# A two-layer attention and expert kernel: own memory for the stacks' parts, late constants, loads of 24 or 25 rows, unread dense products, maxima 13 tiles ahead

## The chip, the cores and the metric

The kernel runs on one core of a Trainium2 chip. The metric is the time of one execution on the device in microseconds (us). Before the change three runs took 2064.13, 2058.0 and 2061.1 us, a median of 2061.1. The profiled execution is a fourth one.

## What is computed

Two transformer layers work on x of shape (2, 1024, 128), all in float32:

```
x = x + attn0(layernorm(x))              # rotary embedding, 16 heads of 8
x = x + ffn0(layernorm(x))               # 1 shared and 7 routed experts, top 2
x = x + attn1(layernorm(x))              # own norm, biases, softmax(q k / sqrt 8) v
x = x + ffn1(layernorm(x))               # relative-position attention, then 32 experts, top 4

def attn0: q, k, v = split(x @ Wqkv); q, k = rope(q), rope(k)
           attn = softmax(q k^T * 8**-0.5); return (attn v) @ Wo
```

For two sequences and 16 heads each attention has 32 (sequence, head) pairs, called heads below. Each has 1024 queries, 1024 keys and a width of 8.

## The kernel before

The program is ten stages, each written once for every engine: `front(0)`, `attention(0)`, `front(1)`, `experts0`, `front(2)` (with `back(0)` ahead of it), `attention(1)`, `front(3)`, `relative_attention`, `front(4)`, `experts1`. Every engine runs its own list in the order written, and semaphores tie the lists together. No scheduler reorders anything. TensorE is `e` under `@block.tensor`, VectorE (DVE) under `@block.vector`, ScalarE (ACT) under `@block.scalar`, GpSimd (POOL) under `@block.gpsimd`; SyncE (SP) issues all DMAs in one queue.

**A front** works on four groups of 512 tokens. DVE normalizes rows, TensorE transposes them, ACT copies the transpose to `XT`, and TensorE multiplies it with the weights (`proj_ok`). In front(0) DVE rotates k and q (L1091 to L1101: two products with `rope`, one sum, each). Every q and k value is split into a rounded high part and a low remainder: ACT writes the high part (`khi_ok`, `qhi_ok`), POOL (front 0, L1690 and L1693) or DVE the low one. These parts live in `hls`, two buffers in turn, the second inside `PR`. `q_out` (L330) and `k_out` (L341) store them to `q_stack` and `k_stack` in DRAM as 24 rows a head; rows 24 to 31 come from `in_pad`, and row 24 of the k stack holds ones.

**An attention's head** is loaded by `load_qk` (L366): eight DMAs of 32 rows, four copies of q and four of k, into slot s of `Qs` and `Ks`. Three things then happen to a head. Its maxima: `scores` (L624, L630) makes a tile of 128 queries by 1024 keys in two of four PSUM banks, and DVE takes the negated row maximum (L1212); eight tiles a head. Its maxima's row: `max_row` (L637) transposes the eight columns, ACT copies them to `MT` (L1474), and `max_rows` (L383) sends them by two DMAs into row 24 of two of the head's q copies, so that the next product has the maximum subtracted already. Its `position`: sixteen `turned` products (L645) with keys along the partitions, ACT's exponentials (L1486), and `values` (L655), three key tiles behind. `scores` may be two tiles ahead of DVE, `turned` three products ahead of ACT. A position starts with the wait for its own maxima's row (`m_in`). The lead is two heads: 16 tiles of scores go before position 0, and position n carries the scores of head n+2, one tile for each of its eight steps. In step 1 it has `max_row` for head n+1, and in step 2 it waits until ACT has copied that row.

TensorE begins an attention after `products_read`, that is once every product of the front has been read out of PSUM, and in attention 0 after the constants have come (`c_in`). The constants and the pad rows are issued by SP at the program's start (L320 to L327). ACT's first maxima's row waits until all parts are stored (`stacks_stored`), because `PR` holds some of them.

Of the kernel before, what the change touches and what calls it, by code (L numbers as in the profile page):

```python
# [24 lines left out]
P = 128  # L25
# [62 lines left out]
def two_layers(nc, A, out):  # L88
    with ExitStack() as ctx:
# [79 lines left out]
        kin = [qk[:, 1, :], PR[:, 2, 0:GW]]  # L169
        hl0, hl0_r = two("hl", [P, 2, 2, GW])  # L170
        hls = [hl0_r, PR_r[:, 0:2, :].rearrange("p a (b t) -> p a b t", b=2)]
# [60 lines left out]
        qin_ok = sem("qin_ok")  # L232
        kin_ok, split_q, lgt_ok, ex_in, ex_ok, gate_ok, gtp_ok, gt_ok = map(
# [14 lines left out]
        pad_in, khi_ok, qhi_ok = map(sem, "pad_in khi_ok qhi_ok".split())  # L248
# [38 lines left out]
        RING = [0, 1, 7]  # L287
        TURN = [[0, 1], [4, 5]]
        FIRST = [2, 0, 4]
        MEETINGS = [3, 4, 9, 10]  # L290
        GATE_BANK = [3, 5, 1, 2]
        EARLY = (0, GT * (NG - 1))
# [18 lines left out]
        def _(e):  # L311
# [8 lines left out]
            for d, src, w in ((q_stack, 0, L), (k_stack, 1, L), (w_stack, 0, 2 * P)):  # L320
                e.dma_start(d[:, MROW:KR, :], A["pad"][src:src + 1, :, 0:w].broadcast_to([NH, KR - MROW, w]))\
                    .then_inc(pad_in, 16)
            loads = [(w_qkv[:, 1:3, :], A["w_qkv"][:, 1:3, :]), (w_out[:], A["w_out"]), (cols[:], A["cols"]),
                     (rows[:], A["rows"]), (rel[:], A["rel"][:, 1:3, :]), (w_rt0[:], A["w_rt0"]), (w_rt1[:], A["w_rt1"])]
            for dst, src in loads:
                e.dma_start(dst, src).then_inc(c_in, 16)
            assert len(loads) == N_CONST  # L327

            def q_out(a, g):

                b, half = g // 2, g % 2
                if a == 0:
                    e.wait_ge(split_q, g + 1)
                else:
                    e.wait_ge(qin_ok, 4 * a + g + 1)
                d = q_stack[b * H:(b + 1) * H, :, half * GW:(half + 1) * GW]
                for c in range(TERMS):
                    e.dma_start(d[:, c * DH:(c + 1) * DH, :], hls[g % 2][:, 0, Q_PARTS[c], :].bitcast(F32))\
                        .then_inc(stq_out[half], 16)

            def k_out(a, g):  # L341
# [6 lines left out]
                for c in range(TERMS):  # L348
                    e.dma_start(d[:, c * DH:(c + 1) * DH, :], hls[g % 2][:, 1, K_PARTS[c], :].bitcast(F32))\
# [16 lines left out]
            def load_qk(n, s):  # L366
                for to, of in ((Qs_r, q_stack), (Ks_r, k_stack)):
                    for r in range(4):
                        e.dma_start(to[r * KR:(r + 1) * KR, s, :].bitcast(F32), of[bass.ds(n, 1)].rearrange("n r t -> (n r) t"))\  # L369
                            .then_inc(qk_in[s], 16)  # L370

            def load_rel(n, s):
                load_qk(n, s)
                e.dma_start(Ws_r[WROW, s, :].bitcast(F32), w_stack[bass.ds(n, 1)].rearrange("n r t -> (n r) t")).then_inc(ws_in[s], 16)

            def attention(a):
# [21 lines left out]
                max_rows(0, 0)  # L398
                load(3, 3)
# [4 lines left out]
                position(NH - 3, 1, False)  # L404
                if a == 1:
# [34 lines left out]
            def experts0():  # L440
# [6 lines left out]
                for x in range(1, NE0 - 2):  # L447
                    e.wait_ge(w0_ok, x + 1)
                    load_expert(0, x + 2, x % 2)
                    e.wait_ge(xw_ok, NG * x)  # L450
# [17 lines left out]
            def front(f):  # L468
# [8 lines left out]
                for g in range(NG):  # L477
# [3 lines left out]
                    if g == 2:  # L481

                        for half in range(2):
                            e.wait_ge(stq_out[half], 16 * TERMS * (2 * a + 1))
                            e.wait_ge(stk_out[half], 16 * TERMS * (2 * a + 1))
                        e.wait_ge(pad_in, 16 * 3)
                        if f == 3:
                            e.wait_ge(w_out_ok, 16 * 6)
                            load_rel(0, 0)
                        else:  # L490
                            load_qk(0, 0)
                    q_out(a, g)
                    k_out(a, g)
                    if g == 2:
                        for n in range(1, 3):
                            if f == 3:
                                load_rel(n, n)
                            else:
                                load_qk(n, n)
                if f in QKV:  # L500
                    for half in range(2):
                        e.wait_ge(stq_out[half], 16 * TERMS * 2 * (QKV.index(f) + 1))
                        e.wait_ge(stk_out[half], 16 * TERMS * 2 * (QKV.index(f) + 1))
# [30 lines left out]
        def _(e):  # L534
# [18 lines left out]
            def front(f):  # L553
# [24 lines left out]

                if a is not None:
# [5 lines left out]
                for g in range(NG):  # L585
# [4 lines left out]
                    e.wait_ge(xn_ok, u + 1)  # L590
                    if a2 is None:
                        e.wait_ge(xh_ok, 4 * (f // 4) + g)
                    for t in range(GT):
                        m = transpose(PS[:, 0, t * P:(t + 1) * P], xn[:, t, :])
                    m.then_inc(xT_ok, 1)
# [3 lines left out]
                    if a2 is not None:  # L599
                        products_read(4 * a2 + g)  # L600
                        for w, bk in ((2, 3), (3, 4), (0, 1), (1, 2)):
                            if f == 0 or w % 2 == 0:
                                e.matmul(bank(bk), w_qkv[:, a2, w * P:(w + 1) * P], xT(f, g), start=True, stop=True)\
                                    .then_inc(proj_ok, 1)
                        for t in range(GT):
# [15 lines left out]

            def attention(a):
                HB = NH * a

                def scores(n, s, qt):

                    e.wait_ge(max_done, 8 * (HB + n) + qt + 1)
                    for kh in range(2):
                        rows_ = slice((2 + kh) * KR, (3 + kh) * KR)
# [1272 lines left out]
```

## Time and profile before

| | us |
|---|---|
| median of three runs | 2061.1 |
| profiled execution, its own time | 2062.49 |
| its span, first to last instruction | 2060.5 |
| front 0, to TensorE's first score | 46.4 |
| attention 0, to the last output copy | 322.1 |
| attention 1, from its first score | 331.6 |
| relative attention and the rest after 980.3 | 1080.2 |

The profile's page gives the busy time of each engine, the span in 40 slices, the DMA queues, the chain that ended last and the costliest groups. A row of the timeline gives start and length in us, engine, line, operation, what is written from what, how many instructions, and in brackets the idle time before it with what ended it. "PEld" is a weight load, "SPq" a DMA issue. An f32 product is two instructions.

### The profile page before, as it was taken

The page shows a single profiled execution, that of the slowest core. Times are in us where ns is not written, and L with a number is a line of the kernel's source. Part 1 is how long each engine was busy: PE and PEld are TensorE (multiplying, and loading weights), DVE is VectorE, ACT ScalarE, POOL GpSimd, SP SyncE. Part 2 cuts the span into 40 slices and gives each one's busy share as a digit, 9 for nine tenths or more (in the row PEclk, how much of TensorE's full clock was granted, in tenths as well). Part 3 has the DMA queues.
Part 4 walks back from the last instruction along what each step waited for, and adds up shares of the span by engine and source line. Part 5 has one row for each costly group of instructions (what it writes and reads, how often), then busy time and mean ns, then how long its engine had stood idle before and what let it go on. Part 6 is the DMA issues. An engine that isn't in the chain of part 4 may idle for free.

```text
span 2060.5 us, 40384 instructions
## 1 busy us (share of the span) xinstructions
PE 1918.0 (93%) x13792; PEld 1159.1 (56%) x13792; DVE 1382.8 (67%) x1778; ACT 1205.9 (59%) x2289; POOL 507.2 (25%) x493
## 2 busy tenths in 40 slices
PE   5999999799985999999689999999999999977998
PEld 2333333577762333333356666666666666665887
DVE  6999997556658899996565455555555555346776
ACT  2699999466652799999224444444444444433553
POOL 2000000178862100000222222222222222103654
PEclk8799999899996799999799999999999999988999
DMA  8444542121106445453512211111112211014554
GB/s 275 135 129 127 129 128 77 60 88 63 52 0 196 113 119 134 123 136 86 170 52 60 58 48 50 47 48 47 47 51 61 51 50 47 8 33 179 213 218 144
DMA packets 90189, 198.58 MB, mean 96 GB/s; under 512 B 19872, under 2 KB 49312, under 8 KB 84768
## 3 DMA queue, kind: packets, MB, share of 16 engines
q1 hardware_dynamic: 90080, 197.10, 32.5%
q8 instruction: 71, 1.16, 0.2%
q14 instruction: 38, 0.31, 0.1%
HBM read 162.42 MB, written 36.18 MB: 96 GB/s over the span
## 4 chain that ended last, share of the span: by engine, by line
PE 46%; DVE 2%; DMA 1%; SPq 1%; issue 0%; ACT 0%; DVEq 0%
PE PS L749 17%; PE PS L833 8%; PE PS L761 6%; PE PS L735 6%; PE PS L744 4%; PE PS L724 4%; DVE M L1233 1%; SPq L369 1%; DMA Ks<-in_kv 0%; DMA Ws_r<-w_stack 0%; PE PS L768 0%; PE PS L575 0%; PE PS L707 0%; PE PS L566 0%; PE PS L545 0%
## 5 line engine op out<-in xcount | busy, mean ns | idle before, releaser
L1212 DVE TENSOR_REDUCE M<-PS 128x1 f32<-128x1024 f32 x512 | 595.1, 1217 | 23.0 <-PE PS L630 17.6
L1486 ACT ACTIVATE PR<-PS 128x512 f32<-128x512 f32 x1024 | 539.2, 602 | 41.7 <-PE PS L645 21.3
L1522 ACT ACTIVATE PR<-PS 128x512 f32<-128x512 f32 x512 | 305.8, 598 | 378.5 <-PE PS L749 374.7
L1233 DVE TENSOR_REDUCE M<-PS 128x1 f32<-128x1024 f32 x256 | 311.8, 1221 | 218.4 <-PE PS L735 211.3
L655 PE MATMUL PS<-PR,Va 128*32 128x256 f32 x4096 | 332.2, 397 | 15.6 <-POOL Va L1669 2.7
L645 PE MATMUL PS<-Qs_r,Ks_r 32*128 32x512 f32 x1024 | 310.6, 508 | 0.5 <-ACT PR L1486 0.4
L630 PE MATMUL PS<-Ks_r,Qs_r 32*128 32x512 f32 x1024 | 269.6, 524 | 23.0 <-DVE M L1212 10.3
L630 PEld LDWEIGHTS PS<-Ks_r,Qs_r 32*128 32x128 f32 x1024 | 99.6, 192 | 228.4 <-issue 153.2
L1228 DVE TENSOR_TENSOR rt<-PS,rel 128x512 f32<-128x512 f32 x128 | 88.4, 691 | 162.5 <-PE PS L707 160.9
L655 PEld LDWEIGHTS PS<-PR,Va 128*32 128x32 f32 x4096 | 83.5, 108 | 149.7 <-ACT PR L1486 62.0
L1669 POOL TENSOR_TENSOR Va<-Vt,nil 128x64 f32<-128x64 f32 x96 | 27.8, 293 | 536.7 <-PE PS L655 533.3
L749 PE MATMUL PS<-BIG_r,Eh 128*128 128x512 f32 x512 | 159.4, 393 | 0.0
L1750 POOL TENSOR_TENSOR qk<-rt 128x512 f32<-128x512 f32 x64 | 82.4, 1287 | 277.9 <-DVE rt L1228 277.9
L645 PEld LDWEIGHTS PS<-Qs_r,Ks_r 32*128 32x128 f32 x1024 | 133.1, 185 | 26.7 <-ACT PR L1486 11.1
L1776 POOL TENSOR_TENSOR BIG_r<-BIG,BIG_r 128x512 fp32r<-128x512 f32 (+1 forms) x96 | 128.3, 1342 | 49.0 <-ACT BIG_r L1554 48.7
L761 PE MATMUL PS<-PR,Va 128*32 128x256 f32 x2048 | 136.8, 385 | 0.0
L1289 DVE TENSOR_TENSOR BIG<-PS,SRC 128x512 f32<-128x512 f32 (+1 forms) x96 | 65.9, 688 | 86.0 <-PE PS L833 85.8
L833 PE MATMUL PS<-Ah,PR_r 128*128 128x512 f32 x376 | 116.4, 391 | 0.0
L833 PE MATMUL PS<-BIG_r,PR_r 128*128 128x512 f32 x384 | 108.0, 390 | 4.5 <-POOL BIG_r L1814 3.3
L749 PEld LDWEIGHTS PS<-BIG_r,Eh 128*128 128x128 f32 x512 | 96.1, 188 | 21.3
L749 PE MATMUL PS<-BIG_r,El 128*128 128x512 f32 x256 | 101.1, 395 | 0.0
L749 PE MATMUL PS<-Ah,Eh 128*128 128x512 f32 x256 | 100.8, 394 | 0.0
(204 smaller groups left out, 3034.8 us busy)
## 6 DMA issues: line engine op xcount, KB each, us to landing
Qs_r<-q_stack SPq DMA_DIRECT2D x384, 128.0 KB, 2.6
Ks_r<-k_stack SPq DMA_DIRECT2D x384, 128.0 KB, 3.1
Qs<-g_dram SPq DMA_DIRECT2D x29, 1024.0 KB, 4.7
o_dram<-Ob SPq DMA_DIRECT2D x96, 128.0 KB, 2.0
Ks<-g_dram SPq DMA_DIRECT2D x10, 1024.0 KB, 4.8
q_stack<-hl_r SPq DMA_DIRECT2D x18, 256.0 KB, 3.3
k_stack<-hl_r SPq DMA_DIRECT2D x18, 256.0 KB, 4.1
q_stack<-PR_r SPq DMA_DIRECT2D x18, 256.0 KB, 3.2
```

What stands on the lines that cost most here:

```text
L630: m = e.matmul(bank(2 + 2 * (qt % 2) + kh), Qs_r[rows_, s, qt * P:(qt + 1) * P], Ks_r[rows_, s, kh * GW:(kh + 1) * GW], start=True, stop=True)
L645: e.matmul(bank(RING[(x + turn) % 3]), Ks_r[rows_, s, kt * P:(kt + 1) * P], Qs_r[rows_, s, qh * GW:(qh + 1) * GW], start=True, stop=True). ...
L655: m = e.matmul(PS[32 * g:32 * g + VC, 6, 0:256], Va[:, s, kt, :], PR[:, kt % 4, g * 256:(g + 1) * 256], start=(kt == 0), stop=(kt == QT - 1))
L735: m = e.matmul(bank(bk + kh), q[:, qt * P:(qt + 1) * P], k[:, kh * GW:(kh + 1) * GW], start=first, stop=not first)
L749: m = e.matmul(bank(TURN[kt % 2][qh]), e_part[:, kt * P:(kt + 1) * P], a_part[s][:, qh * GW:(qh + 1) * GW], start=False, stop=(k == 2))
L761: m = e.matmul(PS[32 * g:32 * g + VC, 6, 0:256], Va[:, s, kt, :], PR[:, kt % 4, g * 256:(g + 1) * 256], start=(kt == 0), stop=(kt == QT - 1))
L833: m = e.matmul(out, w[a], h[b], start=start and n == 0, stop=n == 2 or not start, skip_group_check=not start)
L1212: e.tensor_reduce(M[:, s, qt:qt + 1], PS[:, 2 + 2 * (qt % 2):4 + 2 * (qt % 2), :] .rearrange("p a b -> p (a b)"), AX.X, ALU.max, negate=Tr ...
L1233: e.tensor_reduce(M[:, s, qt:qt + 1], PS[:, bk:bk + 2, :].rearrange("p a b -> p (a b)"), AX.X, ALU.max, negate=True).then_inc(max_done, 1)
L1486: e.activation(PR[:, kt % 4, qh * GW:(qh + 1) * GW], bank(RING[(x + turn) % 3]), ACT.Exp, scale=SCALE).then_inc(exp_done, 1)
L1522: e.activation(PR[:, kt % 4, qh * GW:(qh + 1) * GW], bank(TURN[kt % 2][qh]), ACT.Exp)\
L1776: e.tensor_tensor(h0p[0:w, 1, tg % 2, c, :], h0[0:w, c, :], h0p[0:w, 0, tg % 2, c, :].bitcast(F32), ALU.subtract).then_inc(lo_ok, 1)
```

## The change

1. The parts of front 0 get four buffers of their own in `BIG`, those of front 2 three of four; `stacks_stored` goes from attentions 0 and 1.
2. In front 0 POOL takes over the two sums of the rotation, TensorE transposes group g+1 in the middle of group g's products, and ACT copies that transpose ahead of group g's parts.
3. The constants are issued at the end of attention 0, the pad rows in experts0. Only the row of ones is sent at the start.
4. In attentions 0 and 1 q is loaded with 24 rows, k with 25, and the products use 24 (scores) or 25 rows (turned). Heads 0 and 1 are loaded ahead of group 2's stores, head 2 ahead of group 3's.
5. `keep_warm` multiplies weights by weights into PSUM that nobody reads: 26 products of 128 columns before attention 0's first score, 28 before attention 1's, one of 256 columns after each of the 13 leading tiles, and one in each of the first three steps of position 0.
6. The lead is 13 tiles (NEAR = 5 of head 1). Position n carries tiles 5 to 7 of head n+1, then 0 to 4 of head n+2. `max_row` moves from step 1 to step 4, the wait for its copy from step 2 to step 5, and ACT's copy from before exponential 4 to before exponential 10.

```diff
+        wide = BIG_r[:].rearrange("p (g a b t) -> p g a b t", g=NG, a=2, b=2)
+        PAIR = [hl0_r, PR_r[:, 0:2, :].rearrange("p a (b t) -> p a b t", b=2)]
+        HL = {0: [wide[:, g] for g in range(NG)],
+              2: [hl0_r, wide[:, 2], wide[:, 3], hl0_r],
+              3: [PAIR[g % 2] for g in range(NG)]}
...
SP:
-            for d, src, w in ((q_stack, 0, L), (k_stack, 1, L), (w_stack, 0, 2 * P)):
+            def constants():      # 7 DMAs, at the end of attention 0
+            def pads():           # 3 DMAs, in experts0
+            e.dma_start(k_stack[:, MROW:MROW + 1, :], ...).then_inc(one_in, 16)
...
-            def load_qk(n, s):
+            def load_qk(n, s, q_depth=MROW, k_depth=MROW + 1):
...
                 max_rows(0, 0)
+                if a < 2:
+                    stored(2 * (a + 1))
                 load(3, 3)
...
                 position(NH - 3, 1, False)
+                if a == 0:
+                    constants()
...
TensorE, front 0:
+                            if f == 0 and w == 0:
+                                if g + 1 < NG:
+                                    turn_rows(g + 1)
+                                e.wait_ge(qrot_ok, g)
...
+            def keep_warm(n, bk=7, cols_=256):
+                for _ in range(n):
+                    e.matmul(PS[:, bk, 0:cols_], w_qkv[:, 0, 0:P], w_qkv[:, 0, 0:cols_], start=True, stop=True)
...
TensorE, position:
                     for kt in range(QT):
-                        if ahead:
-                            if kt == 0:
+                        if kt < QT - NEAR and n + 1 < NH:
+                            scores(n + 1, (s + 1) % SLOTS, NEAR + kt)
+                        if kt >= QT - NEAR and n + 2 < NH:
+                            if kt == QT - NEAR:
                                 e.wait_ge(qk_in[s2], ...)
-                            scores(n + 2, s2, kt)
+                            scores(n + 2, s2, kt - (QT - NEAR))
                         turned(n, s, 2 * kt, turn)
                         turned(n, s, 2 * kt + 1, turn)
-                        if kt == 2 and rows_next:
+                        if first and kt in FREE6:
+                            keep_warm(1, 6)
+                        if kt == 5 and n + 1 < NH:
                             e.wait_ge(mt_copied, HB + n + 2)
...
-                        if kt == 1 and rows_next:
-                            max_row(n + 1, (s + 1) % SLOTS, alone=first)
+                        if kt == 4 and n + 1 < NH:
+                            max_row(n + 1, (s + 1) % SLOTS)
...
+                keep_warm([26, 28][a], cols_=P)
                 products_read(4 * (a + 1))
-                if a == 0:
-                    e.wait_ge(c_in, 16 * N_CONST)
                 for n in range(2):
                     e.wait_ge(qk_in[n], 128 * (NH // SLOTS * a + 1))
-                    for qt in range(QT):
+                    for qt in range([QT, NEAR][n]):
                         scores(n, n, qt)
+                        keep_warm(1)
...
ACT:
-                        if x == 4 and rows_next:
+                        if x == 10 and rows_next:
                             max_copy(n + 1, (s + 1) % SLOTS)
...
-                stacks_stored(a)
+                if a == 0:
+                    e.wait_ge(split_k, NG)
+                    e.wait_ge(split_q, NG)
...
POOL, front 0:
+                        e.tensor_tensor(kin[g % 2], rt[:, 0, :], rt[:, 1, :], ALU.add).then_inc(kin_ok, 1)
+                        e.tensor_tensor(qk[:, 0, :], rtq[:, 0, :], rtq[:, 1, :], ALU.add).then_inc(qin_ok, 1)
```

TensorE's list where front 0 ends and attention 0 begins, before (L606 is the last product of the front, L630 the scores, L637 the maxima's row, L645 the turned products, L655 the values):

```order
L606 MATMUL PS<-w_qkv,XT 128x128 x4
L630 MATMUL PS<-Ks_r,Qs_r 128x512 x20
L637 MATMUL PS<-ident,M 8x128
L630 MATMUL PS<-Ks_r,Qs_r 128x512 x14
L645 MATMUL PS<-Qs_r,Ks_r 128x512 x2
```

The same place in the changed kernel (L649, L678 and L685 are the same functions; L668 is `keep_warm`):

```order
L649 MATMUL PS<-w_qkv,XT 128x128 x4
L668 MATMUL PS<-w_qkv 128x128 x26
L678 MATMUL PS<-Ks_r,Qs_r 128x512 x2
L668 MATMUL PS<-w_qkv 128x256
L678 MATMUL PS<-Ks_r,Qs_r 128x512 x2
```

The dense products stand ahead of the first score and between the tiles; 13 tiles go before the first turned product instead of 16 (a 17th stood in position 0's first step).

TensorE's list in position 0, before, from the last leading tile on:

```order
L630 MATMUL PS<-Ks_r,Qs_r 128x512 x14
L645 MATMUL PS<-Qs_r,Ks_r 128x512 x2
L630 MATMUL PS<-Ks_r,Qs_r 128x512 x2
L645 MATMUL PS<-Qs_r,Ks_r 128x512 x2
L637 MATMUL PS<-ident,M 8x128
L630 MATMUL PS<-Ks_r,Qs_r 128x512 x2
```

and after, steps 2 to 5 of position 0 (L693 turned, L703 values):

```order
L668 MATMUL PS<-w_qkv 128x256
L678 MATMUL PS<-Ks_r,Qs_r 128x512 x2
L693 MATMUL PS<-Qs_r,Ks_r 128x512 x2
L703 MATMUL PS<-PR,Va 32x256 x4
L678 MATMUL PS<-Ks_r,Qs_r 128x512 x2
L693 MATMUL PS<-Qs_r,Ks_r 128x512 x2
L703 MATMUL PS<-PR,Va 32x256 x4
L685 MATMUL PS<-ident,M 8x128
L678 MATMUL PS<-Ks_r,Qs_r 128x512 x2
```

The row of the next head's maxima stands three steps later in a position than it did.

SP's list around the first loads, before:

```order
L349 DMA k_stack<-PR_r 16x8x512 x3
L369 DMA Qs_r<-q_stack 32x1024 x4
L369 DMA Ks_r<-k_stack 32x1024 x4
L338 DMA q_stack<-hl_r 16x8x512 x3
L349 DMA k_stack<-hl_r 16x8x512 x3
L369 DMA Qs_r<-q_stack 32x1024 x4
```

and after:

```order
L366 DMA k_stack<-BIG_r 16x8x512 x3
L386 DMA Qs_r<-q_stack 24x1024 x4
L386 DMA Ks_r<-k_stack 25x1024 x4
L386 DMA Qs_r<-q_stack 24x1024 x4
L386 DMA Ks_r<-k_stack 25x1024 x4
L355 DMA q_stack<-BIG_r 16x8x512 x3
```

Head 1's loads now stand ahead of group 2's stores, and each DMA has fewer rows.

## Rows read from the trace of the kernel before

**Rows 1.** The page, part 2: granted TensorE clock in 40 slices of 51.5 us.
```profile
PEclk8799999899996799999799999999999999988999
```
**Rows 2.** Windows, by stage: stretch, us, busy of PE, PEld, DVE, ACT, POOL, clock, DMA share, GB/s.
```profile
46.40:368.50 322.10, 308.41 (x3140) 120.10 (x3141) 298.06 (x257) 284.11 (x577) 12.67 (x41) 0.96 0.46 123
648.70:980.30 331.60, 313.70 (x3140) 120.83 (x3141) 298.85 (x257) 284.51 (x577) 17.55 (x34) 0.93 0.47 127
```
**Rows 3.** Windows inside the two attentions.
```profile
46.35:74.30 27.95, 22.14 (x88) 7.82 (x88) 25.25 (x22) 8.06 (x15) 4.54 (x13) 0.51 0.59 170
74.30:349.00 274.70, 267.23 (x2870) 104.54 (x2867) 271.80 (x234) 258.33 (x527) 8.18 (x28) 1.00 0.47 123
...
648.70:669.00 20.30, 12.47 (x34) 4.56 (x34) 18.28 (x16) 1.55 (x2) 0.42 (x1) 0.50 0.86 256
669.00:695.60 26.60, 24.20 (x156) 7.59 (x160) 16.95 (x14) 15.74 (x31) 9.23 (x7) 0.50 0.36 97
```
**Rows 4.** Timeline of DVE at attention 0's start.
```profile
46.92 20.45 DVE L1212 TENSOR_REDUCE M<-PS 128x1 f32<-128x1024 f32 x18 [1.90 <-PE PS L630]
67.72 2.35 DVE L1212 TENSOR_REDUCE M<-PS 128x1 f32<-128x1024 f32 x2 [0.35 <-PE PS L630]
```
**Rows 5.** Timeline of DVE at attention 1's start.
```profile
649.57 9.14 DVE L1212 TENSOR_REDUCE M<-PS 128x1 f32<-128x1024 f32 x8 [2.63 <-PE PS L630]
...
671.78 2.35 DVE L1212 TENSOR_REDUCE M<-PS 128x1 f32<-128x1024 f32 x2 [2.90 <-PE PS L630]
```
**Rows 6.** Timeline of front 0: a group's value products, POOL, first loads, first score.
```profile
24.14 1.05 PE L606 MATMUL PS<-w_qkv,XT 128*128 128x128 f32 x8
...
27.34 1.26 POOL L1693 TENSOR_TENSOR PR_r<-qk,PR_r 128x512 fp32r<-128x512 f32 x1 [1.29 <-ACT PR_r L1396]
...
28.28 3.70 PE L603 MATMUL PS<-XT,w_qkv 128*128 128x512 f32 x8 [2.65 <-ACT XT L1438]
...
35.68 1.74 SPq L369 DMA_DIRECT2D Qs_r<-q_stack  x4
...
46.38 0.74 PE L630 MATMUL PS<-Ks_r,Qs_r 32*128 32x512 f32 x4 [3.43 <-DVEq L1208]
```
**Rows 7.** Timeline of front 2: first loads, last product, first score of attention 1.
```profile
641.99 1.73 SPq L369 DMA_DIRECT2D Qs_r<-q_stack  x4
...
643.58 1.05 PE L606 MATMUL PS<-w_qkv,XT 128*128 128x128 f32 x8
...
648.74 1.22 PE L630 MATMUL PS<-Ks_r,Qs_r 32*128 32x512 f32 x4 [4.10 <-DMA Ks_r<-k_stack]
```
**Rows 8.** Timeline of attention 0's end.
```profile
339.67 9.48 DVE L1212 TENSOR_REDUCE M<-PS 128x1 f32<-128x1024 f32 x8
...
366.16 1.93 PE L655 MATMUL PS<-PR,Va 128*32 128x256 f32 x32
```
**Rows 9.** Timeline of one position in the middle of attention 0.
```profile
207.20 1.72 SPq L369 DMA_DIRECT2D Qs_r<-q_stack  x4
...
207.45 0.50 PE L630 MATMUL PS<-Ks_r,Qs_r 32*128 32x512 f32 x2
...
209.56 0.38 PE L637 MATMUL PS<-ident,M 128*8 128x128 f32 x2
...
210.20 0.25 ACT L1474 ACTIVATE MT<-PS 8x128 fp32r<-8x128 f32 x1
...
212.18 1.34 SPq L383 DMA_DIRECT2D Qs_r<-MT  x2
...
216.84 0.50 PE L630 MATMUL PS<-Ks_r,Qs_r 32*128 32x512 f32 x2
```
**Rows 10.** Windows at the loads' end and after that row's DMAs (columns of group 2).
```profile
213.00:213.50 0.50, 0.50 (x9) 0.16 (x8) 0.50 (x1) 0.50 (x3) 0.00 (x0) 1.00 0.18 55
214.50:214.75 0.25, 0.25 (x7) 0.13 (x3) 0.25 (x1) 0.25 (x2) 0.00 (x0) 1.00 0.04 12
214.75:215.00 0.25, 0.25 (x4) 0.21 (x4) 0.25 (x1) 0.25 (x2) 0.00 (x0) 1.00 0.00 0
```
**Rows 11.** DMA queue from 641 to 652: packets, MB, share of 16 engines.
```profile
q1 hardware_dynamic: 1266, 2.66, 79.9%
```

More of the change, by code:

```diff
@@ L319, in _ @@
             e.dma_start(rope[:], A["rope"]).then_inc(rope_in, 16)
-            for d, src, w in ((q_stack, 0, L), (k_stack, 1, L), (w_stack, 0, 2 * P)):
[L321 to L327, printed above, removed]
+            def constants():
+                loads = [(w_out[:], A["w_out"]), (cols[:], A["cols"]), (rows[:], A["rows"]),
+                         (w_rt0[:], A["w_rt0"]), (w_rt1[:], A["w_rt1"]),
+                         (w_qkv[:, 1:3, :], A["w_qkv"][:, 1:3, :]), (rel[:], A["rel"][:, 1:3, :])]
+                for dst, src in loads:
+                    e.dma_start(dst, src).then_inc(c_in, 16)
+                assert len(loads) == N_CONST
+            def pads():
+                for d, src, w in ((q_stack, 0, L), (k_stack, 1, L), (w_stack, 0, 2 * P)):
+                    e.dma_start(d[:, MROW:KR, :], A["pad"][src:src + 1, :, 0:w].broadcast_to([NH, KR - MROW, w]))\
+                        .then_inc(pad_in, 16)
+            e.dma_start(k_stack[:, MROW:MROW + 1, :], A["pad"][1:2, 0:1, 0:L].broadcast_to([NH, 1, L])).then_inc(one_in, 16)
             def q_out(a, g):
@@ L481, in front @@
                     if g == 2:
[L483 to L486, printed above, removed]
+                        stored(2 * a + 1)
                         if f == 3:
+                            e.wait_ge(pad_in, 16 * 3)
                             e.wait_ge(w_out_ok, 16 * 6)
@@ L490, in front @@
                         else:
+                            e.wait_ge(one_in, 16)
                             load_qk(0, 0)
+                            load_qk(1, 1)
+                    if g == 3 and f < 3:
+                        load_qk(2, 2)
                     q_out(a, g)
                     k_out(a, g)
-                    if g == 2:
+                    if g == 2 and f == 3:
                         for n in range(1, 3):
[L496 to L503, printed above, removed]
+                            load_rel(n, n)
+                if f == 3:
+                    stored(2 * (QKV.index(f) + 1))
             def attention1():
@@ L577, in spread, with turn_rows @@
                     m.then_inc(spread_ok, 1)
+                def turn_rows(g):
+                    e.wait_ge(xn_ok, 4 * f + g + 1)
+                    if a2 is None:
+                        e.wait_ge(xh_ok, 4 * (f // 4) + g)
+                    if f == 0:
+                        e.wait_ge(xs_ok, g)
+                    for t in range(GT):
+                        m = transpose(PS[:, 0, t * P:(t + 1) * P], xn[:, t, :])
+                    m.then_inc(xT_ok, 1)
+                if f == 1:
+                    e.wait_ge(c_in, 16 * N_CONST)
                 if a is not None:
@@ L589, in front @@
                         spread(3)
[L590 to L595, printed above, removed]
+                    if f > 0 or g == 0:
+                        turn_rows(g)
                     if g:
@@ L657, in values, with position @@
                     m.then_inc(pv_done, 1)
-                def position(n, block, s, turn, first=False, ahead=True, rows_next=True):
+                def position(n, block, s, turn, first=False):
                     s2 = (s + 2) % SLOTS
@@ L693, in attention @@
                 for n in range(1, NH):
-                    position(n, n // SLOTS, n % SLOTS, n % 3, ahead=n < NH - 2, rows_next=n < NH - 1)
+                    position(n, n // SLOTS, n % SLOTS, n % 3)
                 for kt in range(QT - 3, QT):
@@ L1402, in projected @@
                         else:
[L1403 removed]
+                            e.activation(HL[f][g][:, 1, 0, :], bank(3), ACT.Copy).then_inc(khi_ok, 1)
                         e.wait_ge(proj_ok, pr + 2)
[L1405 removed]
+                        if f == 3:
+                            e.wait_ge(stq_out[half], 16 * TERMS * (2 * a2 + g // 2))
+                        elif g == 3:
+                            e.wait_ge(stq_out[0], 16 * TERMS * (2 * a2 + 1))
```

98 lines of the change are left out of this document (59 added, 39 removed).

## The prediction

> **What bounds the kernel now.** I read the page's clock line first, because TensorE's clock decides which engine is the bound. In [rows 1] it has a low slice at the start and another at slice 13, counted from 1; at 51.5 us a slice these are the beginnings of the two attentions. The windows by stage come next: [rows 2] give 322.1 us to attention 0 and 331.6 to attention 1, with equal work and clocks of 0.96 and 0.93. Then I cut each attention [rows 3]. From 74.3 to 349.0 the clock is 1.00 and VectorE is busy 271.80 of 274.70 us with 234 maxima, TensorE 267.23, ACT 258.33: three engines in lockstep, 274.70 / 234 × 8 = 9.39 us a head. Before 74.3 the clock is 0.51; from 648.7 to 695.6 it is 0.50, so TensorE ran at 1.2 GHz, not 2.4. There VectorE waits. Last come timelines. VectorE has gaps in both slow stretches [rows 4, 5]. TensorE's first score comes at 46.38, right after the front's last product is read [rows 6], and at 648.74, after a wait of 4.10 us for the first head's loads [rows 7]. At the end the last maximum is taken at 339.67 + 9.48 = 349.15, and the values end at 368.1: 19.0 us in which VectorE has no maxima [rows 8].
>
> So an attention costs its 256 maxima on VectorE (one every 9.39 / 8 = 1.17 us), the gaps at its start, and the tail. The change touches all three and hardly the other stages.
>
> **The change part by part**, summed against the profiled execution's 2062.5 us, which is 1.4 above the median of the three runs.
>
> *Attention 0's start.* The first loads wait for the stores of groups 0 and 1. POOL ends group 1's last part at 27.34 + 1.26 = 28.6, and the loads are issued from 35.68 [rows 6], 7.1 later. Own buffers remove waits of ACT for earlier stores, but POOL gets two more operations a group; at 1.26 each, four are 5.0 us a group. I put group 1's parts at 28.2 to 30.2 and the loads at 35.3 to 37.3. In front 2 a head is there 648.74 − 641.99 = 6.75 us after its first issue [rows 7]: 42.0 to 44.0. TensorE's front may end near 37, since POOL's sums overlap the next group. The 26 dense products follow. Four value products, also of 128 columns (eight instructions), took 1.05 us, 0.26 each; four of 512 columns took 3.70, which is 0.23 for 128 [rows 6]. So 26 are 6.0 to 6.8 us and end at 43 to 43.8. I take the first score at 43.3: −3.0. Bounds: −4.5 (loads at 35.3, no dense product late) and +0.5 (group 1 late behind POOL's five us a group).
>
> *Attention 0's slow stretch.* Of 27.95 us VectorE worked 25.25; 0.57 is the wait for the first tile, so some 2.1 to 2.3 are gaps [rows 3, 4]. With TensorE kept busy they go: at full clock a tile's scores (0.50, [rows 9]) and one dense product of 256 columns (2 × 0.23) are 0.96, under VectorE's 1.17. What is late next is the maxima's row of head 0, for which I keep 0.3: −2.0. Bounds −2.3 and +3.0 (the slow clock stays in part).
>
> *Attention 1's start.* TensorE waited 4.10 us for the loads there, its last front product ending at 644.6 [rows 7]. 28 dense products at 0.23 are 6.4 us: first score at 651.0, +2.3. Bounds 0 and +3.2 (0.26 each); a little comes back if the loads, now of 24 and 25 rows, are quicker, which doesn't help as the dense products end last.
>
> *Attention 1's gaps.* VectorE worked 18.28 of the first 20.30 and 16.95 of the next 26.60 us: 11.67 idle, less 0.87 for the first tile, 10.8 [rows 3]. They hold 2.90 ahead of 671.78 [rows 5], where ACT's first row waited for the parts' stores, and that wait is gone. I keep 0.7: −10.1. Bounds −10.8 and 0.
>
> *Tail.* The lead is 13 tiles, so after the last maximum there are three tiles' time less. At full clock the tail's 19.0 us are two heads of 16 tiles [rows 8], 1.19 a tile, of which a little is a fixed end; at 1.13 a tile three are 3.4, for each attention: −6.8. Bounds −7.2 and −5.
>
> *Steady state.* The scores and turned products are as many as before, in another order; what moves is the maxima's row. In [rows 9] a position begins at 207.45, ACT's copy at 210.20, 2.75 later; three steps of 1.17 make that 6.26 and its end 6.51. SP is free then: its loads are issued from 207.20, and the queue is nearly empty by 213.0 (share 0.18, [rows 10]). Two issues take 1.34, after some 0.16, and the last packets land 1.15 behind the issue, since 212.18 + 1.34 = 213.52 and the share falls to 0.04 and 0.00 by about 214.65 [rows 10]. The row is home at 6.51 + 0.16 + 1.34 + 1.15 = 9.16, and the next position starts at 9.39 [rows 9]: 0.23 to spare. Behind that wait stand TensorE's scores and turned products, thus VectorE and ACT at once; what covers it is VectorE's tile in hand and ACT's two exponentials, about 0.4. I take 0.05 a head over 60 heads: +3. Bounds −3 (the even mix of tiles runs closer to VectorE's 1.16) and +17.
>
> *Constants.* Seven DMAs at attention 0's end stand in SP's queue ahead of the last output stores, some 2 MB at the 2.66 MB in 11 us of [rows 11], so 8 us, beside two heads of computation: +0.5, bounds 0 and +2. The pad rows go out in experts0 between loads of experts, and I give them nothing: the expert in hand hides them, and uncovered they would cost about 2.25 / 2.66 × 11 = 9 us once. Loads of 24 and 25 rows move 23% less beside compute; nothing, since the queue already empties before a position ends [rows 10].
>
> Sum: −3.0 − 2.0 + 2.3 − 10.1 − 6.8 + 3.0 + 0.5 = −16.1, so 2046.4 for a profiled execution, and 2045.0 against the median.
>
> **Rivals.**
>
> *A. The maxima's row is late in every head.* For: only 0.23 us to spare, by a chain of five terms. Against: up to 0.4 of cover. At 0.3 us a head over 58 heads it takes back 17 us: 2062, the same as before.
>
> *B. The clock doesn't hold, slower than before.* For: in the slow stretch of attention 1 TensorE was busy 24.20 of 26.60 us and its clock was 0.50 all the same [rows 3], so busy time alone doesn't bring the high clock. If it stays low through the leading tiles, a tile is its scores (0.74 then, [rows 6]) and a dense product at half speed (0.92), about 1.7 us against VectorE's 1.13 with no gap: 13 × 0.57 = 7.5 an attention, 15 in both, and the savings of the gaps (12.1) don't come: −16.1 + 27.1 = +11.0, 2072. It decides from the point where the clock is still 0.5 at the sixth or seventh tile. Against: the dense products leave no idle time ahead of the first score, and in the steady state a busy TensorE has 1.00 [rows 3].
>
> *C. Loads of 24 and 25 rows use fewer DMA engines.* Now 32 rows go over 16 engines, a head's 1 MB being 64 KB on each, and [rows 11] give 2.66 MB / 11 us / 0.8 / 16 = 19 KB a us and busy engine: 3.4 us a head. If the rows were spread over 12 and 5 engines, the busiest five would carry 4 × 8 + 4 × 20 = 112 KB, 5.9 us. That lies inside a head's 9.39, so steadily nothing unless the maxima's row has to queue behind it; loads seen from 207.20 on would then end near 214.2, when that row is issued. The first head comes up to 2.5 later in attention 0 (+2.5) and 0.5 in attention 1: 2048. The Trainium skill, "DMA: Bandwidth & Descriptors", section "Why a DMA increments its semaphore by 16 and not by 1", says that the number of engines is the largest up to 16 that divides both sides' outer sizes, which gives 12 for 24 rows and 5 for 25. No row here has a load of 24 or 25 rows.
>
> *D. More gain.* Front 0 by the lower bound, the steady state at −3: 2045.0 − 1.5 − 6 = 2037.5. It belongs to the forecast's range.
>
> **How the numbers follow.** Forecast with D 0.60, A 0.14, B 0.12, C 0.14. A measurement tells about 0.3%, 6.2 us, from no change. Forecast and C lie under 2054.9 but for a small part of each; A is split between the same and a little slower or faster, B is slower. Faster: 0.57 of the forecast, 0.14 of C, 0.03 of A, 0.74. Same: 0.03 of the forecast, 0.08 of A and 0.01 of B, 0.12. Slower: 0.11 of B and 0.03 of A, 0.14. The forecast's own range is 2036 to 2053: the front's, the tail's and the steady state's ends, which are not all met at once. To leave out 2 in 10 it reaches into A, to 2062, and on the low side to 2032 for a steady state better than I can bound. B stays outside.
>
> **What would show it.** Right: the first score near 43 and 651; the clock 1.00 from the first tile or a few later; VectorE's gaps in the first 25 us of each attention under 1 us in all; the last maximum to the end of values 15.6 us instead of 19.0; a head in the steady state 9.39 to 9.45. Wrong: TensorE idle at a position's start with the wait for the row's DMA named there (A); 0.5 in the windows of the leading tiles (B); a DMA share near 5/16 while a head is loaded (C). The forecast fails if a steady head is above 9.6 or the leading 13 tiles take over 19 us.

## The result and the profile after

The change made the kernel slower. Sixteen runs have a median of 2094.6 us (2066.0 to 2113.0) against 2064.8 of the kernel before (16 runs, 2058.0 to 2069.3); the ratio is 1.011 with a 95% interval of 1.009 to 1.013, taken without the five longest runs, whose clocks were lowest (0.937 to 0.944), while the two medians are 1.4% apart. Time and mean granted clock go together over the runs: 0.968 at 2066.0 us, 0.953 at 2088.2, 0.937 at 2113.0. The profiled run took 2106.1 us (span 2104.3, clock 0.941), so the sizes read from it are those of a longer run.

Where the 43.8 us between the two spans (2104.3 and 2060.5) lie, read from the timelines:

| us | before | after | difference |
|---|---|---|---|
| first score of attention 0 | 46.4 | 44.3 | −2.1 |
| to attention 0's last maximum | 302.8 | 327.9 | +25.1 |
| its tail, to the last values | 18.9 | 15.6 | −3.4 |
| to attention 1's first score | 280.6 | 287.2 | +6.6 |
| to attention 1's last maximum | 312.2 | 327.4 | +15.2 |
| its tail | 18.9 | 15.6 | −3.4 |
| the rest | 1080.6 | 1086.3 | +5.7 |

The clock line of the page, beside [rows 1], is low over two slices at the start of each attention (slices 2 and 3, 13 and 14, counted from 1, of 52.6 us each); the low slice 21 lies behind attention 1, as slice 20 did before:

```profile
PEclk9579999799998599999979999999999999988999
```

The windows (columns as in [rows 2]), cut where the clock changes:

```profile
44.30:60.00 15.70, 14.27 (x54) 6.40 (x54) 14.79 (x13) 1.55 (x2) 2.77 (x8) 1.00 0.78 271
60.00:128.30 68.30, 66.88 (x440) 20.55 (x440) 45.31 (x37) 42.35 (x82) 1.17 (x4) 0.50 0.22 69
128.30:365.00 236.70, 231.74 (x2457) 93.30 (x2456) 228.71 (x200) 219.87 (x451) 7.04 (x24) 1.00 0.31 98
675.03:677.80 2.77, 2.77 (x11) 1.38 (x12) 2.24 (x2) 0.00 (x0) 0.00 (x0) 1.00 1.00 336
677.80:735.80 58.00, 58.00 (x284) 20.09 (x283) 39.12 (x33) 25.44 (x48) 9.92 (x8) 0.50 0.35 113
735.80:957.70 221.90, 216.58 (x2296) 87.09 (x2294) 213.98 (x188) 205.47 (x421) 6.76 (x23) 1.00 0.32 100
957.70:967.90 10.20, 10.20 (x74) 2.94 (x70) 6.95 (x6) 6.76 (x14) 0.29 (x1) 0.50 0.24 78
```

Attention 0 starts as forecast: 13 maxima in 15.7 us at 2.4 GHz. Then come 68.3 us at 1.2 GHz in which VectorE takes 37 maxima; at 1.17 us each they would need 43.3, so 25.0 are lost. Attention 1 loses 58.0 − 33 × 1.17 = 19.4, and 10.2 − 6 × 1.17 = 3.2 in a third stretch. Before, the stretches at 1.2 GHz were 27.3 and 47.8 us long, and the first of them lay mostly over the lead, where VectorE still set the pace: its 22 maxima in 27.95 us [rows 3] lost 27.95 − 22 × 1.17 = 2.2. Now TensorE, not VectorE, is the bound: busy 58.00 of 58.00 us in attention 1, and the clock stays down.

What stood ahead of the first fall, from the timeline of TensorE and SP:

```profile
55.13 0.39 PE L685 MATMUL PS<-ident,M 128*8 128x128 f32 x2
...
55.93 1.90 SPq L406 DMA_DIRECT2D Qs_r<-MT  x2
...
57.99 0.70 PE L668 MATMUL PS<-w_qkv 128*128 128x256 f32 x2
...
61.42 0.79 PE L678 MATMUL PS<-Ks_r,Qs_r 24*128 24x512 f32 x2 [2.73 <-DMA Qs_r<-MT]
```

Head 0's maxima's row is made after the tenth tile, at 55.13. Three tiles follow, and TensorE then stands 2.73 us until the row is home at 61.4. The clock falls at 60.0, inside that wait. The other two falls have a wait ahead of them as well, in attention 1 for the first head (fall at 677.8), in its steady state for a row (957.38 is a position's start, the fall is at 957.7):

```profile
665.16 2.63 SPq L386 DMA_DIRECT2D Qs_r<-q_stack  x4
...
675.03 0.49 PE L678 MATMUL PS<-Ks_r,Qs_r 24*128 24x512 f32 x2 [1.27 <-DMA Ks_r<-k_stack]
...
678.53 0.79 PE L678 MATMUL PS<-Ks_r,Qs_r 24*128 24x512 f32 x2
679.25 1.22 PE L668 MATMUL PS<-w_qkv 128*128 128x256 f32 x2
...
957.38 0.55 PE L678 MATMUL PS<-Ks_r,Qs_r 24*128 24x512 f32 x2 [1.14 <-DMA Qs_r<-MT]
```

The view of TensorE's waits (us in total, times, longest) has seven for the row; before there was one, of 3.5 us.

```profile
PE PS L678 <- DMA Qs_r<-MT: 6.9, 7, 2.7
```

### The profile page after: what moved, and what is told of

It is laid out like the page before. It is cut to its first block, busy times and chain, and to the rows that moved or that the text cites. A ratio compares the mean times of both kernels' runs of the same rounds, so it can differ in the third digit from the quotient of the medians.

```text
span 2104.3 us, 40783 instructions
## 1 busy us (share of the span) xinstructions
PE 1987.1 (94%) x13964; PEld 1197.7 (57%) x13964; DVE 1372.9 (65%) x1770; ACT 1206.8 (57%) x2289; POOL 517.8 (25%) x501
## 4 chain that ended last, share of the span: by engine, by line
PE 46%; DVE 2%; DMA 1%; SPq 1%; issue 0%; ACT 0%; DVEq 0%
PE PS L801 17%; PE PS L885 8%; PE PS L787 6%; PE PS L813 6%; PE PS L796 4%; PE PS L776 4%; SPq L386 1%; DMA Ks<-in_kv 0%; DVE M L1280 0%; DMA Ws_r<-w_stack 0%; PE PS L820 0%; PE PS L600 0%; PE PS L759 0%; PE PS L591 0%; DMA k_stack<-PR_r 0%
## 5 line engine op out<-in xcount | busy, mean ns | idle before, releaser
L703 PE MATMUL PS<-PR,Va 128*32 128x256 f32 x4096 | 351.6, 418 | 7.1 <-POOL Va L1726 3.4
L693 PE MATMUL PS<-Qs_r,Ks_r 25*128 25x512 f32 x1024 | 326.3, 532 | 0.1
L678 PE MATMUL PS<-Ks_r,Qs_r 24*128 24x512 f32 x1024 | 277.4, 537 | 8.4 <-DMA Qs_r<-MT 6.9
L678 PEld LDWEIGHTS PS<-Ks_r,Qs_r 24*128 24x128 f32 x1024 | 101.9, 196 | 231.6 <-issue 112.6
L703 PEld LDWEIGHTS PS<-PR,Va 128*32 128x32 f32 x4096 | 85.2, 111 | 145.2 <-issue 69.0
L693 PEld LDWEIGHTS PS<-Qs_r,Ks_r 25*128 25x128 f32 x1024 | 141.3, 193 | 22.1 <-ACT PR L1542 6.2
L813 PE MATMUL PS<-PR,Va 128*32 128x256 f32 x2048 | 136.8, 385 | 0.0
L1881 POOL TENSOR_TENSOR BIG_r<-BIG,BIG_r 128x512 fp32r<-128x512 f32 x64 | 82.6, 1292 | 73.7 <-ACT BIG_r L1676 71.7
```

What stands on the lines that cost most here:

```text
L678: m = e.matmul(bank(2 + 2 * (qt % 2) + kh), Qs_r[rows_, s, qt * P:(qt + 1) * P], Ks_r[rows_, s, kh * GW:(kh + 1) * GW], start=True, stop=True)
L693: e.matmul(bank(RING[(x + turn) % 3]), Ks_r[rows_, s, kt * P:(kt + 1) * P], Qs_r[rows_, s, qh * GW:(qh + 1) * GW], start=True, stop=True). ...
L703: m = e.matmul(PS[32 * g:32 * g + VC, 6, 0:256], Va[:, s, kt, :], PR[:, kt % 4, g * 256:(g + 1) * 256], start=(kt == 0), stop=(kt == QT - 1))
L813: m = e.matmul(PS[32 * g:32 * g + VC, 6, 0:256], Va[:, s, kt, :], PR[:, kt % 4, g * 256:(g + 1) * 256], start=(kt == 0), stop=(kt == QT - 1))
```

## The experiments

Three theories had to be told apart: the row of maxima comes late and the stall brings the clock down (ROW), products of 24 or 25 rows keep it down longer (ROWS24), the dense products lengthen the lead (DENSE). Each ratio below is to the kernel before, with its 95% interval. One run of each kernel was profiled. The stages behind attention 1 are the same in all kernels, and yet took 1076.9 to 1087.3 us in the profiles (1080.6 before); what two whole spans differ by is therefore not all due to the edit.

**1. The lead of 16 tiles again**, in the changed kernel.

```
NEAR = 8;  max_row in step 1, its wait in step 2;  ACT's copy ahead of exponential 4;  FREE6 = (0, 1)
```

> The changed kernel with its sixth point undone: 16 leading tiles, the maxima's row back in step 1 (two of the three extra dense products in position 0 stay). Theory ROW (the row of maxima comes home after the next position starts, TensorE stalls, its clock falls to 1.2 GHz): no wait for the row's DMA in the steady state, no slow stretch inside an attention, 2050 to 2062 us, with attention 0 at 2.4 GHz from its start. Theory ROWS24 (products of 24 or 25 rows make a slow stretch last longer): slow stretches at the attentions' starts stay at 50 to 70 us, 2080 to 2095. Theory DENSE (the dense products at 1.2 GHz lengthen the lead): little changes, about 2090.

Measured: 2072.9 us, ratio 1.004 (1.001 to 1.008). Attention 0 had no slow stretch, and TensorE waited for no row. Attention 1 had one of 75.1 us, which began 1.4 us after a wait of 1.16 us ahead of position 0. Between the theories: the stalls for rows go, the length of a stretch doesn't.

**2. 32 rows again**, in the changed kernel.

```
def load_qk(n, s, q_depth=KR, k_depth=KR);  rows_ of scores and turned over KR = 32 rows;  pads() at the start
```

> The changed kernel with loads and products of 32 rows in attentions 0 and 1 again, and the pad rows at the program's start, as before the change. Theory ROWS24: once in a position, the 1.2 GHz stretch ends within 7 to 25 us, as before the change; stretches of 30 to 45 us instead of 58 and 68; 2065 to 2075 us. Theory ROW: the stalls at the positions' starts stay or grow a little, as a head's loads are longer, and with them the slow stretches: 2085 to 2105.

Measured: 2066.3 us, ratio 1.000 (0.998 to 1.003): the rows alone give back the whole loss. Eight waits for the row, 9.4 us in all, the longest 3.7: no fewer than with 24 rows. But the stretches that follow are 6.8 and 10.2 us long. From the windows, the lead and the slow stretch of attention 0, then of attention 1:

```profile
46.00:64.60 18.60, 16.35 (x66) 7.57 (x66) 16.34 (x15) 3.06 (x5) 2.08 (x6) 1.00 0.92 274
64.60:71.40 6.80, 6.80 (x38) 2.34 (x36) 4.49 (x4) 4.18 (x9) 0.00 (x0) 0.50 0.44 101
...
654.00:672.20 18.20, 14.54 (x57) 6.52 (x56) 14.79 (x13) 1.55 (x2) 1.83 (x3) 1.00 1.02 320
672.20:682.40 10.20, 10.08 (x48) 3.95 (x48) 6.12 (x5) 5.70 (x11) 7.54 (x4) 0.50 0.27 68
```

**3. No dense products**, in the changed kernel.

```
FREE6 = ();  no keep_warm ahead of the first score or between the tiles
```

> The changed kernel without any dense product. Theory DENSE (they keep TensorE busy without raising its clock, at 1.87 us a tile where VectorE needs 1.2): the lead runs at VectorE's pace, 15 us less in attention 1, about 2080 us. Theory ROW: TensorE idles at the start as before the change and is at 1.2 GHz from the first tile, the 13 leading tiles go by VectorE, then positions run at 1.74 us a tile till the clock comes back; 2085 to 2110, no better than with them.

Measured: 2085.0 us, ratio 1.013 (1.006 to 1.019). Slow from 44.1 for 58.0 us, in attention 1 from 661.9 for 30.7 and from 962.3 for 6.8; waits for the row of up to 5.0 us. By the time DENSE falls: without them it is no better, as the interval takes in the changed kernel's. (In its profile attention 1 needs 311.0 us to the last maximum, 16.4 less than in the changed kernel's, but that one was a longer run.) In one place its mechanism is there all the same. In the changed kernel's attention 1 the ten leading tiles behind the fall come every 1.87 us (678.53 to 680.40), the dense products included, and lose 697.79 − 678.53 − 10 × 1.17 = 7.6 us up to position 0; before, at the same clock, VectorE took a leading tile every 9.14 / 8 = 1.14 us [rows 5].

**4. 24 and 25 rows alone**, in the kernel before; **5. the same with the loads left at 32 rows.**

```
4: to[r*KR : r*KR + depth], of[n, 0:depth];  rows_ over MROW = 24 (scores) and MROW + 1 (turned)
5: only the two rows_
```

> The kernel before the change, with nothing but the loads of 24 and 25 rows and products of as many. Theory ROWS24: the slow stretches at the attentions' starts grow from 27 and 48 us to 50 to 70, 2075 to 2090 us. Theory ROW: nothing changes, 2058 to 2069, as the loads end before a position does.

> The kernel before the change, its loads left at 32 rows, only the products of attentions 0 and 1 over 24 (scores) or 25 rows (turned). This parts the products' rows from the loads'. Theory PRODUCTS (fewer rows in the array hold the clock down longer): as with both, slow stretches of 50 to 80 us at the attentions' starts, 2080 to 2095 us. Theory LOADS (loads of 24 or 25 rows land later or disturb something): no change from before, 2058 to 2070.

Measured: 2094.7 us, ratio 1.012 (1.007 to 1.018), and 2077.4 us, 1.008 (1.004 to 1.011). The row count alone gives a loss as large as the whole change's (four runs in 4), and most of it comes with the products. Whether the loads add something to the time stays open, as the intervals overlap. The slow stretches of 4, then of 5, each with attention 0's first; before they were 27.3 and 47.8 us:

```profile
46.70:125.20 78.50, 71.33 (x428) 22.16 (x428) 59.40 (x50) 39.95 (x77) 5.25 (x16) 0.50 0.30 94
667.90:725.90 58.00, 44.96 (x244) 14.50 (x244) 41.01 (x35) 22.50 (x43) 9.66 (x7) 0.50 0.41 132
```

```profile
49.50:110.90 61.40, 56.18 (x325) 17.75 (x326) 48.52 (x42) 30.50 (x59) 3.77 (x12) 0.50 0.44 117
660.40:745.70 85.30, 73.08 (x440) 22.92 (x440) 60.47 (x52) 40.69 (x79) 10.40 (x10) 0.50 0.49 136
```

**13, 14. One of the two products with fewer rows**, in the kernel before.

```
13: scores over MROW rows;  14: turned over MROW + 1 rows
```

> The kernel before the change, with only the products of the scores over 24 rows instead of 32 (loads and turned products as before). Theory PRODUCTS, in proportion: scores lose 8 of 32 rows, turned products 7 of 32, so each alone lengthens the slow stretches by about half of what both did; 2066 to 2075 us. Rival: only one of the two matters; then this one or the next is at 2058 to 2068 as before and the other at 2072 to 2095.

> The kernel before the change, with only the turned products over 25 rows instead of 32. Theory PRODUCTS, in proportion: about half of the loss, 2066 to 2075 us; the slow stretches at the attentions' starts end 10 to 25 us later than the 27 and 48 us of before. Rival: see the run before.

Measured: 2067.2 us, ratio 1.003 (1.001 to 1.005), and 2065.6 us, 1.001 (0.999 to 1.003). In both profiled runs, the quickest of ten each, the stretches were 34.1 and 41.0 us, 75.1 together, as in the kernel before. Each alone costs a third of the 0.8% of both or less, and for 14 the interval takes in no change: not in proportion, and not one of the two.

**6. One more tile of lead; 7. the hole filled; 8. constants early**, all in the changed kernel with 32 rows.

```
6: NEAR = 6;  max_row in step 3, its wait in step 4;  ACT's copy ahead of exponential 8
7: keep_warm(8) ahead of position 0's first wait
8: constants() at the program's start
```

> The changed kernel with 32 rows, as in the second experiment, and NEAR = 6: 14 leading tiles, and the maxima's row one step earlier in a position (step 3 instead of 4, ACT's copy ahead of exponential 8 instead of 10). Theory ROW: the row is home some 1.2 us earlier against the next position's start, the waits for it in the steady state go (9.4 us in all with NEAR = 5), one more tile in each tail costs 1.2 us, the hole before position 0 shrinks by about a tile: 2058 to 2064 us. Rival: the waits are jitter of single DMAs that is longer than 1.2 us and stay; then 2066 to 2069.

> The changed kernel with 32 rows and eight more dense products of 256 columns between the last leading tile and position 0, where TensorE waited 3.69 us for head 0's row in attention 1 before its clock fell. Theory HOLE (that idle time is what brings the clock down): the clock stays at 2.4 GHz over the start of both attentions, 6.8 and 10.2 us of slow stretch go, some 4 to 6 us less: 2058 to 2063. Rival: the clock falls anyway, because the lead itself is too light: no change, 2063 to 2069.

> The changed kernel with 32 rows and the constants at the program's start, as before the change. From the last values of attention 0 to the first score of attention 1 the change takes 286.6 us with late constants and 32 rows, 280.6 before. Theory LATE (front 1 waits for the constants): 1 to 3 us come back there, and attention 0 begins up to 3 us later: 2063 to 2067 us in all. Rival: that stretch doesn't move, since it is the clock in front 1 and the dense products before attention 1 that lengthen it: 2066 to 2070.

Measured: 6, 2053.8 us, ratio 0.995 (0.993 to 0.997), three waits for the row instead of eight, 5.8 us instead of 9.4, and stretches at 1.2 GHz of 6.8 and 23.9 us in the profile, the longest of its seven runs. That is 12.5 us below experiment 2 and below both ranges: more than the waits explain. 7, 2060.7 us, 0.998 (0.996 to 0.999), no stretch at 1.2 GHz inside an attention (1.00 from 26.3 to 374.5 and from 637.3 to 978.7); one more run, of 2919.3 us at a clock of 0.575, is not in it and stays unexplained. 8, 2063.6 us, 1.000 (0.998 to 1.002): no difference that can be told, 285.4 us between the attentions against 286.6.

**9, 10. Both mends together, with 32 rows and with 24 and 25; 12. the filled hole with a lead of 16 tiles and 32 rows.**

```
9: 2 + 6 + 7;   10: 6 + 7, rows as changed;   12: 1 + 2 + 7 with two dense products in position 0
```

> The changed kernel with 32 rows, NEAR = 6 (14 leading tiles, the maxima's row a step earlier) and the eight dense products ahead of position 0: the two mends of the sixth and seventh experiment together. If both causes (the row's lateness in the steady state, the hole ahead of position 0) are real and separate, their gains add to 2048 to 2053 us, below the kernel before by 10 or more. If NEAR = 6 gained by closing the hole only, the sum is that of the sixth alone, 2052 to 2056.

> The same two mends, but with the change's 24 and 25 rows in loads and products. Theory PRODUCTS-A (fewer rows only delay the clock's return, and don't bring it down): with no hole there is nothing to return from, so no more than 5 us above the kernel with 32 rows, about 2053 to 2058 us, with single runs in which a stall still starts a long slow stretch. Theory PRODUCTS-B (products of 24 and 25 rows also let the clock fall without a hole): slow stretches of 50 us and more stay, 2075 to 2095.

> The changed kernel with 32 rows, the eight dense products, and the lead of 16 tiles with the row back in step 1. Against the same kernel with NEAR = 6 it shows what the shorter lead is worth: by the tails, two tiles in each attention, 2 x 2 x 1.19 = 4.8 us, so 2053 to 2058 us. Rival: at NEAR = 6 the row is still late at times and eats the tail's gain; then the two are equal within 2 us.

Measured: 9, 2049.8 us (2048.1 to 2054.7), ratio 0.993 (0.990 to 0.995), the best version. Both attentions run at 2.4 GHz from the first score to the last maximum, 256 maxima each:

```profile
45.50:348.40 302.90, 295.59 (x3026) 121.98 (x3030) 295.32 (x256) 265.55 (x546) 10.50 (x35) 1.00 0.52 134
650.40:953.80 303.40, 295.63 (x3027) 122.02 (x3030) 295.38 (x256) 265.47 (x546) 17.57 (x34) 1.00 0.51 136
```

In its profile, 12.4 us below that of the kernel before, attention 1 gains 8.8 and the tails 4.4, the stretch between the attentions loses 4.7, and 3.1 come after attention 1, where nothing was changed. Against the profile of 7, the same kernel with one tile less of lead, it is 10.6 us shorter, but 9.8 of these lie behind attention 1; so what the one tile is worth by itself isn't shown.

10, 2066.2 us (2057.4 to 2094.5), ratio 1.000 (0.998 to 1.002). Its profiled run, 2060.6 us, has no slow stretch in an attention (302.5 and 303.8 us at 1.00); the longest run, at a clock of 0.950, may have had some. So PRODUCTS-B falls for the profiled run, and the 5 us of PRODUCTS-A were too few. Its profile is 10.7 us above that of 9, of which 7.8 lie behind attention 1 and none inside the attentions; what the middle runs lose is not seen in a trace. 12, 2060.9 us, 0.998 (0.996 to 0.999): 11 us above 9, where the tails explain 18.9 − 16.7 = 2.2 in each attention; its profile has 5.2 us more after attention 1, where the two programs are equal. In these profiles the shorter lead is thus worth 4 to 6 us, as expected, and the rest lies in other stages.

**11. The dense products alone**, in the kernel before: 26 and 28 before the first scores, one after each of the 16 leading tiles, eight before position 0.

> The kernel before the change with the dense products alone (26 and 28 before the first scores, one after each of the 16 leading tiles, eight before position 0), everything else as it was. Theory GAPS (the gain foreseen for the slow stretches is there, 2 us in attention 0, 10 in attention 1, less 2 to 4 for the dense products before the first score): 2052 to 2058 us. Rival: attention 1's hole before position 0 (3.5 us, the row waits for the parts' stores) is longer than the eight products, the clock falls there as before: 2060 to 2066.

Measured: 2066.9 us, ratio 1.000 (0.998 to 1.002). Attention 1 gained 312.2 − 305.8 = 6.4 us, attention 0 nothing (303.0), although its clock was 1.00 throughout, and the first scores came 4.6 and 3.1 us later, behind the 26 and 28 products, which takes the gain back.

**15. ACT's wait for the constants moved** from front 1 to attention 0's last output copy, in 9.

> The best version so far (32 rows, NEAR = 6, eight dense products ahead of position 0), with ACT's new wait for the constants moved from the start of front 1 to ahead of attention 0's last output copy. In front 1 ACT's table load of 1.28 us stood before the wait for its data in the kernel before, and behind it in the changed one. Theory TABLE: the table load is early again and front 1 begins some 1.3 us sooner, 2047 to 2051 us, which the profile shows and the time hardly can. Rival: the load stays behind, because its place comes from something else: nothing moves.

Measured: 2051.0 us, ratio 0.995 (0.993 to 0.997), the same as 9. In the profile the table load is early again. The changed kernel first, then this one:

```profile
387.87 0.38 ACT L1526 ACTIVATE Ob<-PS 128x256 f32<-128x256 f32 x1 [0.83 <-PE PS L703]
393.26 1.28 ACT L1485 ACT_TABLE_LOAD   x1 [5.01 <-DVE sd L1055]
```

```profile
363.72 0.38 ACT L1523 ACTIVATE Ob<-PS 128x256 f32<-128x256 f32 x1 [0.87 <-issue]
364.12 1.28 ACT L1482 ACT_TABLE_LOAD   x1
```

1.28 us stood behind the wait for DVE in front 1 and now lie beside it; between the attentions it is 282.8 us against 285.3 in 9.

## Why the prediction was wrong

*The step that failed is the rows.* "Loads of 24 and 25 rows move 23% less beside compute; nothing": the loads were weighed, the products were not. Products of 24 rows need the same time as those of 32, and so do those of 25 (495 ns too). The groups of instructions (busy us, mean ns) in stretches at 2.4 GHz, after (140 to 360 us), then before (100 to 340):

```profile
L678 PE MATMUL PS<-Ks_r,Qs_r 24*128 24x512 f32 x374 | 93.5, 495 | 1.6 <-DMA Qs_r<-MT 1.6
```

```profile
L630 PE MATMUL PS<-Ks_r,Qs_r 32*128 32x512 f32 x410 | 102.6, 495 | 0.0
```

But after a fall TensorE stays at 1.2 GHz longer: 58 to 85 us in experiments 4 and 5, against 27 and 48 before, and 7 and 10 with 32 rows in experiment 2. Experiment 3, with a single stretch of 30.7 us in attention 1, and experiment 6, with 23.9 at 32 rows, show the scatter. This was no term of the sum and no rival, and it is worth the whole loss: 2094.6 us with 24 and 25 rows, 2066.3 with 32. Why fewer rows do it stays open. It takes a fall of the clock to bring it out: with the hole filled and one more tile of lead the 24 and 25 rows are at 2066.2 (experiment 10).

*Attention 0's slow stretch*, −2.0 forecast, was +25.1. The lead ran as forecast; the "0.3" kept for head 0's row was 2.73 us. The row's way home from its product was 55.13 to 61.4, 6.3 us, and the shorter lead left three tiles, 3.2 us (55.45 to 58.69), beside it. The steady chain was worked out term by term, the first row's was not. Experiment 7, which fills this hole at 32 rows, shows it to be a cause of the fall: of experiment 2's stretches of 6.8 and 10.2 us none is left.

*Attention 1's gaps*, −10.1 forecast, were +15.2. Here the dense products ended 1.27 us before the first head was home, and the clock fell 2.8 us after the first score. The head took 675.03 − 665.16 = 9.9 us, not the 6.75 of [rows 7]: head 1's loads now stand right behind it (8.5 us with 32 rows in experiment 9), and loads of 24 and 25 rows are slower themselves (in the old order 7.76 us in experiment 4, and 6.45 to 7.11 with 32 rows in experiments 5, 13 and 14).

*Right:* the first score of attention 0, 44.3 for 43.3; the tails, −3.4 each; the steady head at 2.4 GHz, 236.70 / 200 × 8 = 9.47 and 221.90 / 188 × 8 = 9.44 us against 9.44 forecast. Its +3.0 left out that a slow stretch can follow a late row: one did behind the wait of 1.14 us, and cost 3.2. Rival A was half right: the row was late in 6 of some 60 heads, not in all. With 32 rows and both mends, experiment 9 lands at 2049.8, 4.8 above the forecast of 2045.0. In part that is luck: 14 tiles of lead give 4.4 in the tails for 6.8, attention 0 starts 0.9 earlier for 3.0, and 3.1 of its gain lie behind attention 1.

*Between the attentions* +6.6 came for +2.8 forecast. The ACT table load is 1.3 of it; the clock in front 1, at 1.2 GHz for 10.2 and 17.1 us instead of 6.8 and 13.7, can hold the rest. The +5.7 after attention 1 lie in stages that the change doesn't touch: the profile has 6.8 us at 1.2 GHz at 1026, where it was 3.4 before, and two stretches more, of 6.8 and 3.4 us, at 1077 and 1087. With 1079.5 and 1079.9 us, experiments 1 and 8 have none of the 5.7. Why these stretches come is open.

*Rival B*, 2072, was the right sort: with the clock at 1.2 GHz, TensorE's 1.87 us a leading tile in attention 1 (678.53 to 680.40) stand for the 1.7 worked out, and the 7.6 lost over them for 7.5. (The 0.74 in it was misread: that line of [rows 6] is four instructions, two tiles, ahead of the fall at 47.1; a tile at 1.2 GHz takes 0.79.) But it stopped at the leading tiles, and most of the loss lies in the positions behind them, at 1.74 us a step (72.69 to 74.43): nearly all of it in attention 0, and some 12 of the 19.4 us in attention 1.

*Rival C* came true and cost little. Once a head's loads are issued (949.48), their last part runs at a low share of the 16 engines. In the kernel before the share was high to the end of the loads and then fell away [rows 10]. One line of before, then three of after:

```profile
212.50:213.00 0.50, 0.50 (x4) 0.18 (x1) 0.49 (x2) 0.50 (x3) 0.00 (x0) 1.00 0.87 244
...
950.00:950.50 0.50, 0.50 (x12) 0.21 (x4) 0.50 (x1) 0.34 (x2) 0.01 (x1) 1.00 0.29 98
950.50:951.00 0.50, 0.36 (x8) 0.16 (x8) 0.50 (x2) 0.50 (x2) 0.28 (x1) 1.00 0.29 115
951.00:951.50 0.50, 0.50 (x11) 0.09 (x6) 0.50 (x1) 0.50 (x2) 0.00 (x0) 1.00 0.30 123
```

A share of 0.29 to 0.30 is about five engines of 16. The rule of the Trainium skill ("DMA: Bandwidth & Descriptors", "Why a DMA increments its semaphore by 16 and not by 1"), by which 25 rows go over 5 engines, fits that. Rival C brought no more waits for the row: eight with 32 rows, seven with 24 and 25. The first head of attention 1 came 0.7 to 1.3 us later (experiments 4, 5, 13 and 14), for 0.5 worked out.

## What to carry to other kernels

Taking rows out of a product that takes the same time anyway wasn't free here: the stretches at 1.2 GHz became longer. So look at how long a slow stretch lasts, not only at whether one starts. A shorter lead has to be checked against the first head's chain, which has no earlier work to hide it; here a hole of 2 to 4 us there was filled with eight dense products that nobody reads. What a slow stretch costs depends on the engine that sets the pace in it: 2.2 of 27.95 us where VectorE did, about a third of each microsecond where TensorE did (25.0 of 68.3, 19.4 of 58.0).

## What had not been expected of the hardware

- TensorE busy 58.00 of 58.00 us stayed at 1.2 GHz all that time, dense products of 128 rows among the first 26 us of it. Busy time alone didn't bring the clock back.
- Waits as short as 1.14 to 1.50 us stood 0.3 to 2.8 us ahead of a fall in kernels with 24 and 25 rows (two in the changed kernel, one each in experiments 1 and 3), while one of 1.13 us in experiment 3 had none behind it. With 32 rows three waits of 1.15 to 1.35 us in experiments 2 and 7 had no slow stretch behind them, and one of 1.19 us in experiment 8 had one of 3.4 us. The cases are few; why is open.
- Scores of 24 rows alone cost 0.3%, turned products of 25 rows alone 0.1% with an interval that takes in no loss at all, both together 0.8%.
- A wait that is written ahead of an activation moved a table load of 1.28 us from beside a wait to behind it.
